# Self-attention: maximum chunks copied to bf16 by ScalarE, rotation finished on GpSimd, weights through a ring

## What is computed

```python
q = (x @ wq.T + bq).reshape(Bx, Sx, H, DK).transpose(0, 2, 1, 3)   # 16 heads of 64
k = ...; v = ...                                                   # the same
q, k = _rope(q, k)                       # q * cos + rotate(q) * sin; rotate: (x1, x2) -> (-x2, x1)
scores = jnp.einsum('bhqd,bhkd->bhqk', q, k)
scores = jnp.where(causal[None, None], -jnp.inf, scores)
attn = jax.nn.softmax(scores / math.sqrt(DK), axis=-1)
out = jnp.einsum('bhqk,bhkd->bhqd', attn, v)
x = _layernorm(x + out.transpose(0, 2, 1, 3).reshape(Bx, Sx, H * DV) @ wo.T + bo)
```

## Time and profile before

| | us |
|---|---|
| timed runs, median of 3 | 2363.18 |
| lowest, highest | 2362.79, 2363.85 |
| the profiled execution's span | 2372.0 |
| TensorE busy in it | 1899.1 (80%) |
| VectorE busy | 1573.1 (66%) |
| GpSimd busy | 1175.7 (50%) |
| ScalarE busy | 913.5 (39%) |

### The profile page before, as it was taken

The page is one execution under the profiler, slowest core; times in us unless marked ns, Lnnn a source line. Parts: engine busy times, 40 slices in busy tenths (PEclk is TensorE's granted clock), DMA queues, the critical chain, the costliest instruction groups (busy, mean ns, idle before and its releaser), DMA issues. The chain is left out here.

```text
span 2372.0 us, 41450 instructions
## 1 busy us (share of the span) xinstructions
PE 1899.1 (80%) x16891; PEld 1133.8 (48%) x16891; DVE 1573.1 (66%) x2437; ACT 913.5 (39%) x1273; POOL 1175.7 (50%) x938
## 2 busy tenths in 40 slices
PE   6888879888878888888898898668788788885576
PEld 3444445444344444444444453446566566664332
DVE  6765656657756657666666664166868868778676
ACT  0222222222222222222222223147675775875376
POOL 0455435545544554554455455234555354636247
PEclk8999989999999999999999999769898898898696
DMA  6122122212221121131122111200000000100002
GB/s 208 36 52 57 41 52 57 54 39 50 61 57 41 43 65 41 35 74 37 39 63 47 39 41 32 65 6 7 2 2 7 2 2 2 41 2 2 2 1 71
DMA packets 57406, 93.39 MB, mean 39 GB/s; under 512 B 26624, under 2 KB 39040, under 8 KB 52864
## 3 DMA queue, kind: packets, MB, share of 16 engines
q1 hardware_dynamic: 48000, 90.47, 15.1%
q10 hardware_dynamic: 9216, 0.27, 0.2%
HBM read 52.43 MB, written 4.46 MB: 24 GB/s over the span
## 5 line engine op out<-in xcount | busy, mean ns | idle before, releaser
L780 POOL TENSOR_TENSOR acc<-acc,probs 128x1024 f32<-128x1024 f32 (+3 forms) x320 | 553.8, 1731 | 143.6 <-ACT probs L518 114.7
L518 ACT ACTIVATE probs<-psum 128x1024 f32<-128x1024 f32 (+3 forms) x384 | 290.5, 808 | 642.5 <-PE psum L424 642.5
L416 PE MATMUL psum<-operands 64*128 64x512 f32 (+3 forms) x1536 | 314.2, 514 | 59.5 <-DVE maxes L639 23.3
L639 DVE TENSOR_REDUCE maxes<-psum 128x2 f32<-128x1024 f32 (+1 forms) x224 | 268.4, 1223 | 132.0 <-PE psum L394 121.7
L1322 ACT ACTIVATE onehot<-psum 128x1024 bf16<-128x1024 f32 x320 | 322.9, 1037 | 1.3 <-PE psum L1132 1.3
L1150 PE MATMUL psum<-pieces,onehot 128*128 128x64 bf16 x7680 | 295.9, 201 | 24.5 <-ACT vs L1329 17.8
L1150 PEld LDWEIGHTS psum<-pieces,onehot 128*128 128x128 bf16 x7680 | 267.4, 103 | 89.5 <-issue 47.5
L440 PE MATMUL psum<-probs,vals 128*64 128x512 f32 (+3 forms) x1536 | 294.9, 506 | 4.4 <-POOL probs L761 4.4
L1729 POOL TENSOR_TENSOR vs<-vs,wgt 128x1280 f32<-128x1280 f32 x64 | 156.4, 2443 | 257.4 <-DVE wgt L1573 257.3
L761 POOL TENSOR_SCALAR_AFFINE_SELECT probs<-probs 128x256 f32<-128x256 f32 x256 | 132.1, 528 | 283.1 <-ACT probs L518 283.1
L416 PEld LDWEIGHTS psum<-operands 64*128 64x128 f32 x1536 | 131.5, 186 | 201.8 <-issue 85.6
(11 more groups left out here) (220 smaller groups left out, 3173.9 us busy)
## 6 DMA issues: line engine op xcount, KB each, us to landing
operands<-turned SPq DMA_DIRECT2D x124, 256.0 KB, 4.2
rden<-inverse_rows SPq DMA_DIRECT2D x64, 256.0 KB, 3.8
wqk<-in_wqk SPq DMA_DIRECT2D x16, 512.0 KB, 3.2
wv<-in_wv SPq DMA_DIRECT2D x16, 256.0 KB, 2.6
y<-in_x SPq DMA_DIRECT2D x1, 4096.0 KB, 20.6
wo<-in_wo SPq DMA_DIRECT2D x16, 256.0 KB, 2.6
out<-res SPq DMA_DIRECT2D x16, 256.0 KB, 2.1
xT<-in_xT SPq DMA_DIRECT2D x3, 1024.0 KB, 6.5
```

The source lines that it names most:

```text
L416: nc.tensor.matmul(dst[:, hh, 0:width], ops[n % 2][rows, 1, kt * P:(kt + 1) * P].bitcast(F32), ops[n % 2][rows, 0, a:a + width].bitcast(F3 ...
L518: nc.scalar.activation(probs[u % PBUF][:, :, 0:width], slot("s", n, u)[:, :, 0:width], ACT.Exp, scale=1.0 / D ** 0.5).then_inc(s_exp, 1)
L639: V.reduce_max(maxes[:, :, place_of[0]:place_of[-1] + 1:step], src[:, :, 0:len(parts) * width].rearrange("p h (k q) -> p h k q", q=width), ...
L780: G.tensor_tensor(dst, dst, src, ALU.add).then_inc(s_acc, 1)
```

## The change

- **Maxima.** ScalarE copies each chunk from PSUM to one of three bf16 buffers in SBUF (`copy_chunk`, `chunks`, MBUF = 3), 1024 elements per partition whatever the chunk holds. The copy frees the PSUM slot. VectorE masks and reduces the copy; the mask `later` is bf16 too. ScalarE has nine more instructions per pair, 288 in all.
- **Chunks** are in steps 1 to 4 (three, two, two, two) and not 1 to 5; `negate` is in step 4.
- **Row.** `max_row` of the next pair ends a pair, in step 5, and so does its copy on ScalarE. Step 0 has no row left; in it the weighing of the pair before now stands behind the shifts.
- **Rotation.** All four products go to SBUF: two into `turned`, two into one of two buffers `crossed`; the fourth frees the slot. Subtraction and addition are done by GpSimd (`turn`), behind its masks and additions of the step after. The q/k projections are in steps 1 to 4 of the even pair. `stack` waits for GpSimd's part.
- **Weights and x** are loaded in pieces of 256 KB into a ring of three buffers (`raw`, RAW = 3, `split_order`); each is split by itself. wqk has two pieces, wv one, an x four. The split of wqk moves from step 1 to step 4 of the odd pair; that of x to step 5 of the odd pair (two pieces) and step 0 of the even one after it (two). bqk is loaded once, bv by itself. The first wqk, wv and x lie in `acc`, and `den_rows` shares `rden`, whose reading `spread_sums` waits for.

The diff, cut to its core:

```diff
-CHUNKS_AT = [range(0, 0), range(0, 2), range(2, 4), range(4, 6), range(6, 8), range(8, 9)]
+CHUNKS_AT = [range(0, 0), range(0, 3), range(3, 5), range(5, 7), range(7, 9), range(0, 0)]
+LAST_CHUNKS = max(m for m in range(STEPS) if len(CHUNKS_AT[m]))
...
-FULL_AT = [[("qk", 0), ("qk", 1), ("qk", 2), ("qk", 3), None, None],
+FULL_AT = [[None, ("qk", 0), ("qk", 1), ("qk", 2), ("qk", 3), None],
            [("out", 0), ("out", 1), ("v", 0), ("v", 1), None, None]]
...
-        later = sb("later", [P, P])
+        later = sb("later", [P, P], BF16)
...
+        chunks = [sb(f"chunks{n}", [P, 2, BANK], BF16) for n in range(MBUF)]
...
             elif kind == "max":
-                pe.wait_ge(s_mread, PARTS * (NCH * n + u + 1))
+                pe.wait_ge(s_mcopy, NCH * n + u + 1)
...
             elif kind == "qk":
-                pe.wait_ge(s_rot, QK_UNITS * n + u + 1)
+                pe.wait_ge(s_term, TERMS * (QK_UNITS * n + u + 1))
...
+            def load_piece(kind, n, piece):
+
+                k = pieces[kind, n, piece] - X_PIECES
+                if k >= RAW:
+                    sp.wait_ge(s_split, X_PIECES + k - RAW + 1)
...
-                    if (i + 2) % NG == 0 and (i + 2) // NG + 1 < B:
-                        sp.wait_ge(s_xs, X_PIECES * ((i + 2) // NG + 1))
-                        load_x((i + 2) // NG + 1)
+                if i % NG == 2 and i // NG + 1 < B:
+                    for piece in range(X_PIECES):
+                        load_piece("x", i // NG + 1, piece)
...
+            def copy_chunk(n, c):
+
+                k = NCH * n + c
+                act.wait_ge(s_m, k + 1)
+                if k >= MBUF:
+                    act.wait_ge(s_mread, PARTS * (k + 1 - MBUF))
+                nc.scalar.activation(chunks[k % MBUF][:, :, :], slot("max", n, c)[:, :, :], ACT.Copy).then_inc(s_mcopy, 1)
...
-                act.wait_ge(s_dcol, 32 * n)
+                act.wait_ge(s_norm, n)
...
+                co = crossed[m % 2]
+                for dst, x, b, table in ((tu[:, 0, :], ev, be, cosE), (tu[:, 1, :], od, bo, cosO),
+                                         (co[:, 0, :], od, bo, sinE), (co[:, 1, :], ev, be, sinO)):
                     V.scalar_tensor_tensor(out=dst, in0=x, scalar=b, in1=table[:, tok], op0=ALU.add, op1=ALU.mult)\
                      .then_inc(s_term, 1)
...
-                V.tensor_tensor(tu[:, 0, :], tu[:, 0, :], od, ALU.subtract).then_inc(s_term, 1)
-                V.tensor_tensor(tu[:, 1, :], tu[:, 1, :], ev, ALU.add).then_inc(s_rot, 1)
...
-                dve.wait_ge(s_m, NCH * n + c + 1)
-                src = slot("max", n, c)
+                k = NCH * n + c
+                dve.wait_ge(s_mcopy, k + 1)
+                src = chunks[k % MBUF]
...
+            def turn(i, u):
+
+                m = QK_UNITS * i + u
+                hf, qk = divmod(u, 2)
+                tu = turned[:, :, qk, hf * BANK:(hf + 1) * BANK]
+                pool.wait_ge(s_term, TERMS * (m + 1))
+                G.tensor_tensor(tu[:, 0, :], tu[:, 0, :], crossed[m % 2][:, 0, :], ALU.subtract).then_inc(s_rot, 1)
+                G.tensor_tensor(tu[:, 1, :], tu[:, 1, :], crossed[m % 2][:, 1, :], ALU.add).then_inc(s_rot, 1)
```

More of the change, by code:

```diff
@@ L72, in slot_order @@
     order = [("qk", 0, u) for u in range(QK_UNITS)] + [("v", 0, u) for u in range(V_UNITS)]
-    order += [("max", 0, c) for c in range(NCH)]
+    order += [("max", 0, c) for c in range(NCH)] + [("row", 0, 0)]
     for n in range(PAIRS):
@@ L77, in slot_order @@
             order += [("s", n, 2 * m), ("s", n, 2 * m + 1)]
-            if m == 0:
-                order.append(("row", n, 0))
             if n + 1 < PAIRS:
@@ L89, in slot_order, with split_order @@
                 order.append(("den", n - 1, 0))
+            if m == STEPS - 1 and n + 1 < PAIRS:
+                order.append(("row", n + 1, 0))
     order.append(("den", PAIRS - 1, 0))
     return order + [("out", GROUPS - 1, u) for u in range(OUT_UNITS)]
+def split_order():
+    order = [("x", 0, piece) for piece in range(X_PIECES)] + [("qk", 1, kt) for kt in range(KT)]
+    for i in range(GROUPS):
+        if i + 1 < GROUPS:
+            order.append(("v", i + 1, 0))
+        if i + 2 < GROUPS:
+            order += [("qk", i + 2, kt) for kt in range(KT)]
+        if i % NG == 2 and i // NG + 1 < B:
+            order += [("x", i // NG + 1, piece) for piece in range(X_PIECES)]
+    return order
 def attention(nc, dram, y, psum):
@@ L121, in attention @@
         turned = sb("turned", [P, 2, 2, S])
+        crossed = [sb(f"crossed{n}", [P, 2, BANK]) for n in range(2)]
         ops = [sb(f"operands{n}", [P, 2, S], F32R) for n in range(2)]
@@ L199, in attention @@
         place = {use: k for k, use in enumerate(order)}
+        pieces = {use: k for k, use in enumerate(split_order())}
         def slot(kind, n, u):
@@ L718, in _ @@
                             maximum(n + 1, c)
-                    if m == STEPS - 1 and n + 1 < PAIRS:
+                    if m == LAST_CHUNKS and n + 1 < PAIRS:
                         negate(n + 1)
                     if n == 0 and m == 0:
-                        split_qk(1)
+                        for kt in range(KT):
+                            split_qk(1, kt)
                     if p == 1 and m == 0:
@@ L729, in _ @@
                         row_statistics(i // NG - 1, m)
-                    if p == 1 and m == 1 and i + 2 < GROUPS:
-                        split_qk(i + 2)
+                    if p == 1 and m == 4 and i + 2 < GROUPS:
+                        for kt in range(KT):
+                            split_qk(i + 2, kt)
                     if FULL_AT[p][m]:
@@ L797, in _ @@
             G.memset(first[D:D + 1, :], 1.0).then_inc(s_set, 1)
+            pool.wait_ge(s_set, 6)
+            for u in range(QK_UNITS):
+                turn(0, u)
             for n in range(PAIRS):
+                i, p = divmod(n, 2)
                 for m in range(STEPS):
@@ L2226, in lay_attention @@
     o["ident"] = np.eye(128).astype(bf)
[L2227 removed]
+    o["later"] = np.where(i[None, :] > i[:, None], -1e30, 0).astype(bf)
     o["rot"] = rope_tables()
```

176 lines of the change are left out of this document (99 added, 77 removed).

## The result

The changed kernel takes 2381.69 us (median of 5 runs, 2374.82 to 2386.77) against 2363.18 us before, beside it on the same chip: a ratio of 1.0074 with an interval of 1.0049 to 1.0099. It is slower by 0.7%, where I forecast 1% faster, and lies above the range.

What follows compares the result with a forecast made beforehand. TensorE was taken as the bound, its gaps as what could be won. Plain groups gave 0, x -17, start -6, last pairs -2: -25, span 2347, less 8.8 to the median, 2338 us; range 2290 to 2376.

Steps and rivals of the forecast that it cites:

- The step that failed: Even and odd pairs: TensorE's matmul work without waits, 37.5 and 38.9 us, taken as untouched by the change.
- the 6 for the start and the 2 for the last pairs: Start: VectorE freed sooner by the rotations, -6 us; last pairs: no row in the way, -2 us.
- GpSimd's queue: Rival, chance 0.21: rotation's end late on GpSimd delays stacking; 3 us later gives 2383 us; odd first chunks wait over 3.
- Row behind even pairs: End of the even pair: row matmuls wait 3.2 us for the rotation to free a slot, 1.95 without the lock.
- Row behind odd pairs: End of the odd pair: TensorE waits 3.25 us for the negation, 1.85 without the lock.
- Second scores of step 2: Even pair: the second score unit of step 2 waits 2.4 us for the projection's slot, 1.9 without the lock.
- First copy: Even pair's first projection waits 0.75 us for the first chunk's slot, freed by ScalarE's copy; 0.75 in odd pairs too.
- The lock: VectorE instructions with two SBUF inputs and GpSimd's SBUF reads block each other; without it 3.1 us less per group.
- the rival of quick reductions: Part of the shorter-chain rival, chance 0.25: reductions gain from 2-byte inputs, 0.6 us each; 43 us less, 2295 us.
- the slow mask: Rival, chance 0.12: bf16 mask adds take 0.69 and 0.42 us as today; +21 us, 2359 us.
- The stacking: Odd pair: the first chunk waits 1.0 us for the four DMAs stacking its operands, issued after GpSimd finishes the rotations.
- x, start, end: x loaded in 256 KB pieces: three places costing 35 us become 6 us each, -17; start -6, last pairs -2.

Runs made afterwards that it cites:

- experiment 7: Changed kernel with ScalarE's chunk copies undone, VectorE masking and reducing in PSUM in fp32 as before: 2352.36 us, ratio 0.9928 to the kernel before.
- experiment 1: Changed kernel with three useless matmuls per pair ahead of the row's matmuls: 2346.89 us, ratio 0.9926 to the kernel before.
- Experiments 5 and 6: 5: changed kernel, chunks in steps 1 to 4 as three, three, two, one: 2382.82 us. 6: that plus two useless matmuls ahead of the row: 2370.19 us.
- experiment 5: Changed kernel with chunks in steps 1 to 4 as three, three, two, one: 2382.82 us, ratio 1.009 to the kernel before.
- experiment 10: Changed kernel without ScalarE's chunk copies and with the rotation's last two instructions back on VectorE: 2301.55 us, ratio 0.975 to the kernel before.

## Why the prediction was wrong, point by point

**The step that failed.** "What is left is matmul work that the change doesn't touch: 37.5 and 38.9 us." I carried these through every case. But the same prediction put waits of 3.2 and 3.25 us ahead of the rows, where before 1.3 and 1.7 stood, and reckoned with no lower clock behind them. The waits came (3.9 and 2.9), the clock went to 0.50 behind 27 of the 31, and the 7082 matmuls took 39.8 us more. Without these the stretch would be 1388.1 us; my terms for it give 1410.95 - 17 = 1394, since the 6 for the start and the 2 for the last pairs lie outside it. The rest of the sum was right to 6 us there, and no rival held the term that decided. The earlier trace rows had the hint: a clock of 0.97, not 1.00, with waits of up to 5.6 us. Behind the three of that length the trace of before has 1.06 us for the row in place of 0.64.

**The rival that hit the number.** GpSimd's queue had 2383 us, and 2381.69 was measured. That is chance: its sign was a first chunk of odd pairs that waits over 3 us for the stacking, and in the changed kernel no odd pair waits more than 1.4.

**The waits, against what was measured.** Row behind even pairs 3.2: 3.9. Row behind odd pairs 3.25: 2.9. Second scores of step 2, 2.4: 1.7. First copy 0.75: 0.67. The bias and first-probability waits of the earlier trace rows are gone, as said. Most plain pairs are 44.9 to 45.7 us by the row copies, where 44.2 was forecast; three even ones are 46.7 to 47.0. The odd pairs with the layer norm of a batch, 47.5 us before, are 50.1 to 50.2, and one even pair is 49.0. In that one, from 789.41 to 838.38, the wait in step 2 is 2.66 us, and four score matmuls behind it take 1.68 us where the four ahead of it take 1.13: the clock again.

**The lock** was right, and larger than priced (the product L666 takes 1.23 us free, not the 1.13 that I read): the adds spread from 0.28 to 1.52 us, and the tiny combination L698, on which I put nothing, takes 1.02 us at the end of the chain. It and the copies' latency, not the number of elements, make the gap: in experiment 7 the copies are gone, the combination has a median of 0.29 us, and the row's gap fell to 30 us in all.

**The reductions** stay at 1.22 us for 1024 bf16 elements, 1.23 in fp32 from PSUM; the rival of quick reductions falls. The rule of the Trainium skill (VectorE: DVE Perf Modes, The perf-mode tier table), that a reduction gets no faster mode in bf16, holds here. The mask add, taken at 0.42 and 0.29, measures 0.41 and 0.28 when free: the slow mask falls too.

**The stacking** was over-priced: 1.0 us in each odd pair, measured 18.4 us in 5 places, 16.8 of it in the three even pairs behind a load of x. TensorE arrives later than I reckoned, because it was slow: in experiment 1, where it wasn't, the plain odd pairs wait 0.6 to 1.4 us. Experiments 5 and 6, where it is earlier, pay 56.5 and 60.6 us there, so the mechanism stood and was hidden.

**x, start, end.** The three even pairs behind a split are now 51.4 to 51.9 us, 6.2 above a plain one each; I had said 6. The start brought -1.3 us, not -6: the first row copy is at 50.48 in place of 51.80. I had counted VectorE's work there; I take it that the chunks wait for the stacked operands instead, which no run tested. From the last row copy to cross-attention it is 64.8 us where it was 67.2, 2.4 less; forecast 2.

**From the profile to the median.** I took off 8.8 us, as the profiled execution of before was a long one. Timed executions of the kernel before spread over 27 us on one chip (2348.57 to 2375.80), and the later stages, which the change leaves alone, take 832 to 843 us in the profiles. So the profiles differ by 7.9 us and the timed medians by 18.5; the experiments' ratios go by timed runs.

**Open.** The length of a wait alone doesn't decide whether the clock falls. Ahead of the row the scores were slow behind 3 of 15 waits of 1.80 us and 8 of 15 of 2.05 to 2.13, and not behind the one of 2.35 (all in experiment 5), behind 11 of 15 of 2.0 in experiment 7 and behind all 15 of 3.9 in the changed kernel. What else decides isn't settled by these runs. A run with one wait of varied length at one place would tell more, and wasn't made.

## What to carry to other kernels

A wait on TensorE has two prices, its own length and the slow matmuls behind it; when a change makes waits longer (here from 1.3 and 1.7 us to 3.9 and 2.9), look at the granted clock in the windows behind it before holding matmul work constant. Handing work to idle engines pays only if their share of the chain that the bound engine waits for gets no longer: a second engine adds a handover, and VectorE adds on two SBUF tensors stretch by what is left of GpSimd's instruction. When two parts of a change feed the same chain, undo them together as well as apart.

## What the hardware showed that I had not expected

- The granted clock fell to 0.50 behind single waits of 1.66 to 3.9 us, and less often behind the short ones: behind 4 of 14 of 1.66 (experiment 10), 11 of 15 of 2.0 (experiment 7) and all 15 of 3.9 (the changed kernel). In the changed kernel the first eight scores then took 2.5 to 3.4 us where 1.77 is usual, and the cost, 57 us in 31 pairs, is about half of the waits (105 us) ahead of it.
- Useless matmuls can pay: 88.1 us of them made the kernel 34.8 us shorter; the same ones behind the row made it 81 us longer (85 by the ratios to before).
- A VectorE add of 128x8 elements with both inputs in SBUF took up to 1.02 us beside GpSimd's additions, and its median went from 0.17 to 0.52 us, since the new order puts it there in nearly every pair.
- GpSimd pays too: the first of the rotation's two instructions of 512 elements took a mean 1.52 us (the subtraction L850, 1.33 for the addition L851) where an addition of this form has 1.27, and 2.18 beside a VectorE product.
